# Ten idle TensorE products in each step of a relation-wise graph attention kernel

## The reference

```python
q = x[dst] @ W_Q[r];  k = x[src] @ W_K[r];  v = x[src] @ W_V[r]
logit = (q * k).sum(-1) / 4 + attn_bias[r]
# softmax over the edges that share destination and type, then
out[dst] += softmax(logit) * v          # summed over the types
h = layernorm(out @ out_proj_w.T + out_proj_b + x) * gamma + beta
result = layernorm(x + h)               # (3125, 128) float32
```

## Time and profile before

| | us |
|---|---|
| median of 3 runs | 1296.07 (1294.8 to 1296.49) |
| profiled execution, its span | 1301.8 |
| busy: TensorE products | 938.5 |
| busy: VectorE | 1002.1 |
| busy: ScalarE | 547.3 |
| busy: GpSimd | 763.0 |

### The profile page before, as it was taken

One profiled execution on the slowest core, in us unless ns is written; L12 is line 12 of the kernel. 1 busy time (PEld: TensorE's weight loads), 2 busy tenths in 40 slices (PEclk: granted clock), 3 DMA queues, 4 the chain that ended last, 5 costly groups with the idle time before them and its releaser, 6 DMA issues.

```text
span 1301.8 us, 19088 instructions
## 1 busy us (share of the span) xinstructions
PE 938.5 (72%) x5180; PEld 827.1 (64%) x5180; DVE 1002.1 (77%) x1851; ACT 547.3 (42%) x1044; POOL 763.0 (59%) x859
## 2 busy tenths in 40 slices
PE   9924467866778767877787776877677677666777
PEld 4513456765667656766676765767576666666677
DVE  3656678877878778878878788887788788778996
ACT  5624443444434444444444444444444334343322
POOL 0067666666666666666666666666666666666640
PEclk9956555555555555555555555555555555555555
DMA  8976555554655555555654555655555455555410
GB/s 318 379 216 180 168 159 172 157 160 144 166 159 156 148 157 167 157 139 166 174 161 145 146 164 157 182 140 152 162 168 148 136 140 155 146 141 154 131 48 12
DMA packets 121376, 209.26 MB, mean 161 GB/s; under 512 B 22845, under 2 KB 79546, under 8 KB 121166
## 3 DMA queue, kind: packets, MB, share of 16 engines
q0 software_dynamic: 37632, 102.81, 27.8%
q1 hardware_dynamic: 79602, 92.61, 23.8%
q10 hardware_dynamic: 4032, 12.57, 2.5%
HBM read 176.92 MB, written 30.99 MB: 160 GB/s over the span
## 4 chain that ended last, share of the span: by engine, by line
DVE 36%; issue 28%; another core or an unknown queue 16%; PE 14%; ACT 2%; DVEq 2%; DMA 1%; ACTq 0%; POOL 0%; POOLq 0%; SPq 0%
DVE LT L1324 6%; DVE pool L1416 4%; PE pp L1863 4%; DVE av L666 4%; DVE pool L1387 4%; DVE pool L1288 3%; PE pp L572 3%; DVE pool L1310 2%; PE pp L1807 2%; DVE Tt L1300 2%; DVE Yt L1373 2%; DVE ohn L650 2%; PE pp L1846 2%; DVE Mt L1402 2%
## 5 line engine op out<-in xcount | busy, mean ns | idle before, releaser
L1699 POOL DMA_INDIRECT ring<-KVtab,kvi x784 | 745.6, 951 | 491.0 <-issue 207.3
L1807 PE MATMUL pp<-qwin,pool 128*128 128x128 bf16 x2352 | 293.5, 309 | 73.5 <-issue 53.4
L1863 PE MATMUL pp<-ohn,av 128*128 128x32 f32 x1464 | 328.1, 392 | 20.6 <-issue 18.5
L1863 PEld LDWEIGHTS pp<-ohn,av 128*128 128x128 f32 x1464 | 324.4, 328 | 22.1 <-issue 18.7
L1807 PEld LDWEIGHTS pp<-qwin,pool 128*128 128x128 bf16 x2352 | 262.9, 151 | 112.9 <-issue 111.4
L1310 DVE TENSOR_TENSOR pool<-pp,ring 128x512 f32<-128x512 f32 x196 | 133.5, 681 | 81.9 <-remote 67.3
L909 ACT ACTIVATE Et<-pool 120x512 f32<-120x512 f32 (+1 forms) x66 | 41.6, 630 | 293.2 <-DVE pool L1288 160.5
L1884 PE MATMUL pp<-pool,negb 128*128 128x512 bf16 (+1 forms) x84 | 37.3, 444 | 169.2 <-ACT pool L897 107.4
L882 ACT ACTIVATE pool<-rkb,npid 128x512 bf16<-128x512 bf16 x196 | 139.4, 711 | 36.2 <-DMA rkb<-Ktab 18.9
L1846 PEld LDWEIGHTS pp<-sel,pool 120*128 120x128 f32 (+1 forms) x536 | 129.5, 326 | 38.5 <-issue 38.4
L666 DVE TENSOR_TENSOR av<-ring,pp 128x512 f32<-128x512 f32 x183 | 124.2, 679 | 34.2 <-remote 34.0
(11 more groups left out here) (133 smaller groups left out, 969.1 us busy)
## 6 DMA issues: line engine op xcount, KB each, us to landing
rkb<-Ktab SPq DMA_DIRECT2D x196, 128.0 KB
mk<-Mtab SPq DMA_DIRECT2D x201, 100.2 KB
qwin<-Qfast SPq DMA_DIRECT2D x196, 96.0 KB
KVtab<-pool SPq DMA_DIRECT2D x25, 640.0 KB, 6.3
ring<-KVtab,kvi POOLq DMA_INDIRECT x784
Qfast<-pool ACTq DMA_DIRECT2D x21, 480.0 KB
Qfast<-ring SPq DMA_DIRECT2D x4, 480.0 KB
xs<-in_x_b SPq DMA_DIRECT2D x5, 320.0 KB
```

Source lines behind the costliest of these rows:

```text
L1699: e.indirect_dma_start(kv[:, home(m), j, :], None, KV, bass.IndirectOffsetOnAxis(kvi[:, 4 * q + j:4 * q + j + 1], 0)).then_inc(kv_in[m % 6 ...
L1807: last = e.matmul(pp[2 + m % 2][:, j * C:(j + 1) * C], ohr[:, m % OR, j * C:(j + 1) * C], qwin[:, m % 3, k * C:(k + 1) * C], start=(k == 0 ...
L1863: last = e.matmul(sums_at(f)[:, 0:n], weighed_at(f)[:, j, :], hot_at(f)[:, j, 0:n], start=(j == 0), stop=(j == 3))
```

## The change

In TensorE's program a function `spare(m, n)` is added. It issues `n` products of 512 columns from the bfloat16 matrix `negb` (minus the identity, 128 x 128, repeated four times as the moving operand) with `negb` as weights, into the bank into which `queries(m)` will write. Nobody reads what they leave, since `queries(m)` overwrites the bank. It is called with five products in front of `queries(s + 1)` and with five, for `queries(s + 2)`, behind the node sums, in each of the 193 steps; from `m = 2` on it first waits until VectorE has read the bank's last contents.

```diff
+            def spare(m, n):
+                if m >= 2:
+                    e.wait_ge(q_times_k, m - 1)
+                for _ in range(n):
+                    e.matmul(pp[2 + m % 2][:, :].rearrange("p (k c) -> p k c", c=C), negb[:, :],
+                             negb[:, None, :].broadcast_to([128, 4, 128]), start=True, stop=True)
...
             for s in range(END):
+                spare(s + 1, 5)
                 queries(s + 1)
...
                 for f in range(collected_until(s - 1), collected_until(s)):
                     collect(f)
+                spare(s + 2, 5)
                 n, part = divmod(s, QSTEPS)
                 if part < 6 and n < len(LATER_Q):
                     make_q(n, part)
```

## The result

The changed kernel takes **1335.09 us** (median of 4 runs, 1334.75 to 1337.85) against 1296.28 us (4 runs) for the kernel before beside it: ratio 1.0308, 95% interval 1.0294 to 1.0323, 38.8 us slower. The forecast was 1380 us, 83.7 us slower, with a range of 1265 to 1540.

What follows compares the result with a forecast made beforehand. Late TensorE results were taken to pace the 6.00 us step. Work of 4.75 us over speed 0.85, plus 0.84 standing, gives 6.43; 0.43 more over 193 steps is 83 us, so 1380 us, range 1265 to 1540.

Steps and rivals of the forecast that it cites:

- w: Share of TensorE's work at 2.4 GHz, taken as 0.7; speed is w + (1 - w)/2, so 0.85.
- What bounds the kernel: Step loop: no engine is full; arrival times of TensorE's results pace the others, at 6.00 us a step.
- Price of a product: One 512-column idle product takes 0.428 us at 1.2 GHz or 0.222 at 2.4; ten cost 4.28 or 2.22 a step.
- What the clock gives back: TensorE's present 4.41 us a step becomes 2.53 at 2.4 GHz, all halved except the products of `back`.
- Which clock: TensorE's clock rises behind dense bursts and falls behind standing: a rise per step, a fall in two steps of three.
- `back`'s 0.65 us: The eight products of L1846 take 0.65 us a step and gain nothing from the higher clock.
- The wait at nothing: The added wait behind the node sums is already over, costed at nothing; uncovered, at most 0.7 us a step.
- What stays of the idle time: Of TensorE's 1.59 us standing a step, 0.75 in front of L1884 is filled and 0.84 stays.
- A: Rival: the gathers' pace covers the added work and nothing moves, about 1296 us; chance 0.14.
- B: Rival: results arrive earlier and GpSimd's stop before L1699 shrinks, so faster, about 1256 us; chance 0.16.
- C: Rival: TensorE's clock mostly stays at 1.2 GHz, 1520 us and over; chance 0.15.
- D: Rival: TensorE's mid-burst stops during gathers recur, 0.76 us a step or 147 us more: 1443 us; chance 0.12.

Runs made afterwards that it cites:

- 1290 kind: The two series of runs in which the unchanged kernel before takes 1283 to 1296 us.
- eight: Sixteen idle products a step, eight at each place instead of five, against the kernel before in the 1110 kind: 1274.19 us, ratio 1.1472.
- after_again: The whole change, unedited, run again against the kernel before in the 1290 kind: 1324.21 us, ratio 1.0329.
- 1110 kind: The other four series of runs, in which the unchanged kernel before takes 1109 to 1110 us.
- five_behind: Only the five idle products behind the node sums, with their wait, against the kernel before in the 1290 kind: 1303.16 us, ratio 1.015.
- five_front: Only the five idle products in front of the queries, against the kernel before in the 1290 kind: 1305.98 us, ratio 1.0176.
- before: The kernel before, unedited, profiled in the first series beside the change: median 1296.28 us, profiled span 1301.8 us.

## Why the prediction was off

The direction was right (0.70 given to slower) and the time lay in the range, but the loss was less than half of that forecast. The step that failed is the share w of full clock, taken as 0.7 and measured at 0.8; behind it, the idle time that stays was right in size for a wrong reason. By its own steps:

- **What bounds the kernel.** That late results of TensorE pace the others while no engine is full was right for the 1290 kind: VectorE's and GpSimd's waits for queries are what grew. Why they are late before the change was not seen: in 76 of GpSimd's 79 stops the products had ended and only the increment was late. Where increments are prompt the same kernel runs at the floor of 5.0 us.
- **Price of a product.** 0.222 us forecast, 0.215 measured back to back (`eight`), 0.07 us a step less for ten.
- **What the clock gives back.** 2.53 us of real work a step forecast, 2.50 in `eight`. That `back`'s products gain nothing held: their mean is 381 ns after, 394 before.
- **Which clock: the term that was mis-sized.** I took w = 0.7, "a rise per step, a fall in two steps of three". The clock of 0.90 in 300 to 1200 us is w = 0.8. The sum at that share has 4.75/0.9 = 5.28 us of work, and 5.27 was measured; with its 0.84 it gives 6.12 us and 23 us of loss, where w = 0.7 gave 6.43 and 83. So this one number takes away more than the whole overshoot, and the sum at the right share would have fallen short of the 38.8 us measured. It was steep in w: a tenth of it was 0.31 us a step. I had a ground for a rise in nearly every step and none for how often it falls. The sum also contradicts its own step before: it divides `back`'s 0.65 us by the speed, though they gain nothing. Left out of the division, w = 0.7 gives 0.65 + 4.10/0.85 + 0.84 = 6.31 us, a loss of 61 us instead of 83, and the match of 5.28 with 5.27 becomes 5.21 with 5.27.
- **The wait at nothing.** Held for the change: TensorE stands at most 11.6 us of 900 in front of idle products in `after_again`, and the wait by itself cost nothing in the 1110 kind. In the 1290 kind it was not run by itself, and in `five_behind` TensorE stands 69.5 us at it.
- **What stays of the idle time.** 0.84 us forecast, 0.90 and 0.82 measured. That it fits is luck. The 0.84 was what stood in front of lines other than L1884; of the 0.90 after, 0.79 are stops in mid-burst (0.33 before), and the stands at waits that the prediction meant to keep are down to 0.11. Were it a fixed remainder, `five_front` would need 4.89 + 0.84 = 5.73 us, under the present step, and lose nothing; it loses 1.8%. Standing goes from 1.53 to 1.15 to 0.82 as work comes in, and the step grows all the way.
- **Rivals.** A (1296, the gathers' pace covers it) is false here but is just what happens in the 1110 kind, where the cover is 5.0 us against 4.78 of work; `eight`, with 5.94 us of work, is past the point at which it ends. B is refuted: the results that come sooner (node sums, weights: 78.5 us of waits down to 2.1) are outweighed by the queries. C is refuted by the clock: it was 0.90. The Trainium skill ("TensorE: Matmul & The Clock Gate", "Loop structure matters more than you think") warns that a long wait between products lets the clock fall. The rows agree in sign, clock 0.90 with 0.90 us of standing a step, 0.98 with 0.22, 1.00 with none, but these stands left most of it. D came in part. The stops in mid-burst doubled, from 0.33 to 0.79 us a step, 0.46 of the 0.76 it priced; but they took the place of the stands at waits, and did not come on top of them.

Still open is how the loss divides in the 1290 kind. The waits show that the queries reach VectorE and GpSimd later, and the table of stops that the added ones are for query products that end late, some behind idle products alone and some after stops in mid-burst. No kernel with a looser wait or with narrow products met that kind, so how much of the 0.16 to 0.20 us a step each of these makes, and what the late increments add, was not separated.

## What to carry to other kernels

Idle products do raise TensorE's clock (0.52 to 0.90), and nearly halve what the real work takes, but they pay only if they cost less than they give: here ten cost 2.15 us a step and gave at most 1.9 back (4.41 to 2.50), so at best nothing is won, and six or narrower ones, at lower clocks, cost 0.4 to 0.5% in the 1110 kind. Before an engine's added work is costed, fill it (`eight`) to learn its work and its headroom under the slowest pace: with 4.78 us of work under 5.0 the loss was at most 0.2%, with 5.94 it was 14.7%. Mean headroom is not enough, though: six products left more of it than ten and cost more. When a remainder of idle time is carried into a sum, look at what it is made of on both sides; here its size held and its content did not. Where results are late in the trace although their producer is done, read the increments and not only the instructions, and time the change more than once on different occasions.

## What the runs showed of the hardware

- The same kernel takes 1283 to 1296 us in some series and 1109 to 1110 in others. The records name the chip by a number, and one number stands in a series of each kind, so the traces do not tell what decides.
- In the slower kind TensorE's increments arrive late, those for the queries by 2.0 to 2.5 us in the median and 4.8 to 6.8 at the 90th percentile, three quarters of the late ones while GpSimd has stopped issuing gathers (`before`); the recorded ones of VectorE and ScalarE come after 0.01 us. In the other kind TensorE's for the queries come after 0.01 us too.
- In the slower kind TensorE stops in the middle of bursts that have no wait in them, 54 to 124 times in 900 us and up to 1.8 us at a time in the rows shown; in the other kind no such stop is in the four traces looked at.
- The products of `back`, 24 columns of float32 with 120-row weights, take 381 to 394 ns whether the clock is 0.52 or 0.90.
